# Turning an expert's rows with VectorE's 32x32 blocks and a quadrant exchange by DMA, instead of TensorE's transposes

## What is computed

```python
xn = layernorm(x)
# routing: 8 of 32 experts for each token, at most CAP = 512 slots an expert
buf = zeros(E * CAP + 1, H).at[slot].set(xn[tok])
xe = buf[:E * CAP].reshape(E, CAP, H)                  # 32 x 512 x 256
gu = einsum('ech,eoh->eco', xe, gate_up_proj)          # o = 2 * 128
g, u = minimum(gu[..., :128], 7), clip(gu[..., 128:], -7, 7)
ye = einsum('eci,ehi->ech', silu(g) * u, down_proj)
...
out = x + attention(xn) + routed(ye) + shared(xn)
```

## Time and profile before

| | us |
|---|---|
| median of three runs | 3135.45 (3132.16 to 3135.75) |
| the profiled execution | 3129.23 |
| its span from first to last instruction | 3127.6 |

### The profile page before, as it was taken

How to read it: one execution, slowest core, us unless ns; L and a number is a source line. 1 busy time by engine, 2 the same in 40 slices (tenths; PEclk the granted TensorE clock), 3 DMA queues, 4 the chain that set the end, 5 groups by cost and what they waited for, 6 DMA issues and landing times.

```text
span 3127.6 us, 54519 instructions
## 1 busy us (share of the span) xinstructions
PE 3068.8 (98%) x13443; PEld 1592.7 (51%) x13444; DVE 2624.5 (84%) x2773; ACT 1963.5 (63%) x3797; POOL 2102.4 (67%) x2156
## 2 busy tenths in 40 slices
PE   8999999999899999999999999999999999999998
PEld 3355444555455555555555555555555555555554
DVE  9622444334999999999999999999999999999995
ACT  5511420334677777777777777777777777777775
POOL 5877773011577777777777777777777777777776
PEclk9999999999999999999999999999999999999999
DMA  9821887665888888898888888988898888888887
GB/s 350 331 88 55 310 266 179 204 228 187 229 205 219 217 223 221 220 221 225 218 218 217 219 216 213 262 219 223 220 223 219 221 219 224 211 220 220 206 215 182
DMA packets 319034, 685.21 MB, mean 219 GB/s; under 512 B 120813, under 2 KB 170744, under 8 KB 318608
## 3 DMA queue, kind: packets, MB, share of 16 engines
q1 hardware_dynamic: 289808, 626.48, 76.0%
q0 software_dynamic: 29184, 58.22, 5.8%
HBM read 198.37 MB, written 159.51 MB: 114 GB/s over the span
## 4 chain that ended last, share of the span: by engine, by line
PE 69%; DMA 2%; SPq 2%; DVE 1%; issue 0%; ACT 0%; POOL 0%; DVEq 0%; ACTq 0%; POOLq 0%
PE ea_ps L1155 28%; PE ea_ps L1187 26%; PE ea_ps L1202 9%; PE ea_ps L1168 6%; DMA ea_moved<-ea_blocks 2%; SPq L976 1%; DVE ea_half_max L1282 1%; DVE ea_blocks L1299 1%; DMA out<-ahead_acc 0%; SPq L819 0%; ACT ea_scaled L1249 0%; ACT ea_prob L1237 0%; SPq L826 0%; SPq L959 0%; DVE ea_neg_max L1287 0%
## 5 line engine op out<-in xcount | busy, mean ns | idle before, releaser
L1237 ACT ACTIVATE ea_prob<-ea_ps,ea_neg_max 128x1024 f32<-128x1024 f32 x1024 | 1149.1, 1122 | 313.8 <-DVE ea_neg_max L1287 292.4
L1282 DVE TENSOR_REDUCE ea_half_max<-ea_ps 128x1 f32<-128x1024 f32 x1024 | 1201.8, 1215 | 8.5 <-PE ea_ps L1155 7.4
L1299 DVE STREAM_TRANSPOSE ea_blocks<-ea_prob 128x1792 f32<-128x1792 f32 x512 | 1043.1, 2037 | 2.9 <-DMA ea_moved<-ea_blocks 1.2
L1093 POOL COPY ea_moved<-ea_blocks 32x1792 f32<-32x1792 f32 x512 | 857.1, 1674 | 158.5 <-DVE ea_blocks L1299 49.0
L1155 PE MATMUL ea_ps<-ahead_k_hl,ahead_q_hh 128*128 128x512 f32 x2048 | 852.9, 416 | 12.7 <-ACT ea_prob L1237 12.2
L1187 PE MATMUL ea_ps<-ea_moved,ea_v 128*64 128x512 f32 x3584 | 860.0, 593 | 5.3 <-DMA ea_moved<-ea_blocks 5.2
L1155 PE MATMUL ea_ps<-ahead_k_hl,ahead_q_ll 128*128 128x512 f32 x2048 | 807.5, 394 | 0.0
L1108 POOL TENSOR_TENSOR ahead_acc<-ahead_acc,ea_scaled 128x256 f32<-128x256 f32 x512 | 375.8, 734 | 203.3 <-ACT ea_scaled L1249 67.4
L1249 ACT ACTIVATE ea_scaled<-ea_ps,ea_inv 128x256 f32<-128x256 f32 x512 | 242.2, 473 | 316.8 <-PE ea_ps L1202 312.0
L1187 PEld LDWEIGHTS ea_ps<-ea_moved,ea_v 128*64 128x64 f32 x3584 | 261.7, 137 | 351.9 <-issue 292.9
L1155 PEld LDWEIGHTS ea_ps<-ahead_k_hl,ahead_q_hh 128*128 128x128 f32 x2048 | 387.6, 189 | 85.5 <-ACT ea_prob L1237 19.5
(11 more groups left out here) (112 smaller groups left out, 2563.6 us busy)
## 6 DMA issues: line engine op xcount, KB each, us to landing
ea_moved<-ea_blocks SPq DMA_DIRECT2D x1536, 224.0 KB, 6.2
ahead_k_hl<-k_parts SPq DMA_DIRECT2D x64, 512.0 KB, 8.1
ahead_q_hh<-q_parts SPq DMA_DIRECT2D x128, 256.0 KB, 4.6
ahead_q_ll<-q_parts SPq DMA_DIRECT2D x128, 256.0 KB, 5.7
xbuf<-pr_zeros SPq DMA_DIRECT2D x32, 512.0 KB, 3.8
q_parts<-pr_part_hi SPq DMA_DIRECT2D x64, 256.0 KB, 2.4
q_parts<-pr_part_lo SPq DMA_DIRECT2D x64, 256.0 KB, 2.5
k_parts<-pr_part_hi SPq DMA_DIRECT2D x64, 256.0 KB, 2.4
```

Source lines behind the costliest of these rows:

```text
L1093: nc.gpsimd.tensor_copy(moved[r * 32:(r + 1) * 32, parity, r, :, :, :], blocks[r * 32:(r + 1) * 32, parity, r, :, :, :]).then_inc(diag_don ...
L1237: nc.scalar.activation(prob[:, i % 2, half * 1024:(half + 1) * 1024], ps[:, banks[0]:banks[1], :].rearrange("p b c -> p (b c)"), ACT.Exp, ...
L1282: nc.vector.tensor_reduce(half_max[:, i % 2, half:half + 1], ps[:, banks[0]:banks[1], :], AX.XY, ALU.max).then_inc(max_step, 1)
L1299: nc.vector.transpose(blocks[:, parity, :, j, :, :].rearrange("p c t k -> p t c k"), prob[:, (s["s"] - 1) % 2, 0:MOVED * P].rearrange("p ( ...
```

## The change

The rows of a pair are loaded by one transfer in which a partition holds four consecutive rows (`load_rows`), and the weights by `load_weights`. The first pair is still turned by TensorE. For each later pair, VectorE turns both experts' rows in 32x32 blocks into `blk` (`turn_pair`), two pairs ahead, between the pair's two `hidden` steps; SyncE sends twelve off-diagonal quadrants of `blk` to `xeT` (`exchange`), GpSimd copies the four diagonal ones (`diagonal`). `xeT` and `blk` have two places by pair. TensorE's `gate_up` waits for the weights and, in the pair's first expert, for exchange and diagonal; it reads `xeT` in runs of 32. `down` gets two banks for each place (`2 * q`), so that the attention's first scores wait for expert 30's copy. Loops run over two pairs a turn, with two pairs ahead and two behind written out.

```diff
+def load_rows(sp, scr, ahead, i):
+    sp.dma_start(ahead["xe"][:, :, :, :], scr["xbuf"][bass.ds(i * 2 * CAP, 2 * CAP), :]
+                 .rearrange("(q p t) d -> p q t d", p=P, q=2)).then_inc(ahead["xe_loaded"], 16)
...
     def sync(sp):
...
+        def exchange(i, b):
+            wait_apart(sp, blk_done, i, sp_waits)
+            wait_apart(sp, gu_ready, 2 * (i - 1), sp_waits)
+            for turn in range(1, QD):
+                for a, r in zip(ACROSS, ACROSS[turn:] + ACROSS[:turn]):
+                    sp.dma_start(xeT[r * 32:(r + 1) * 32, b, a, :, :, :, :],
+                                 blk[a * 32:(a + 1) * 32, b, r, :, :, :, :]).then_inc(exchanged[b], 16)
+
+        def body(i, b):
+            if follows(i, 2):
+                wait_apart(sp, blk_done, i + 1, sp_waits)
+                load_rows(sp, scr, ahead, i + 2)
+            if follows(i, 1):
+                exchange(i + 1, 1 - b)
+                for q in range(2):
+                    wait_apart(sp, gu_ready, 2 * i + q + 1, sp_waits)
+                    wait_apart(sp, dn_kept, 2 * i + q + 1, sp_waits)
+                    load_weights(sp, io, ahead, 2 * i + 2 + q, q)
+
+        sp.wait_ge(turned, 2)
+        load_rows(sp, scr, ahead, 1)
         for part in range(2):
             load_k(sp, scr, start, 0, 0, 0, part)
         load_q(sp, scr, start, 0, 0, 0)
-        with sp.Fori(1, E // 2) as i:
-            load(i)
+        over_pairs(sp, body)
     def gpsimd(pool):
+        def diagonal(i, b):
+            wait_apart(pool, blk_done, i, pool_waits)
+            wait_apart(pool, gu_ready, 2 * (i - 1), pool_waits)
+            for r in range(QD):
+                nc.gpsimd.tensor_copy(xeT[r * 32:(r + 1) * 32, b, r, :, :, :, :],
+                                      blk[r * 32:(r + 1) * 32, b, r, :, :, :, :]).then_inc(diag_done, 1)
...
+        def body(i, b):
+            if follows(i, 1):
+                diagonal(i + 1, 1 - b)
+            if not isinstance(i, int) or i:
+                store(i - 1)
...
+    def vector(dve):
+        def turn_pair(i, b):
+            dve.wait_ge(xe_loaded, 16 * i + 16)
+            if not isinstance(i, int) or i > 2:
+                dve.wait_ge(exchanged[b], SENT // 2 * (i - 2 + b))
+                dve.wait_ge(diag_done, QD * (i - 2))
+            for q in range(2):
+                last = nc.vector.transpose(blk[:, b, :, q, :, :, :].rearrange("p r t k j -> p (t k) r j"),
+                                           xe[:, q, :, :].rearrange("p t (k r j) -> p (t k) r j", r=QD, j=32))
+            last.then_inc(blk_done, 1)
...
+        def body(i, b):
+            hidden(i, 0)
+            if follows(i, 2):
+                turn_pair(i + 2, b)
+            hidden(i, 1)
+
+        turn_pair(1, 1)
+        over_pairs(dve, body)
     def tensor(pe):
-        def gate_up(i, q):
+        def gate_up(i, q, b):
             n = 2 * i + q
-            pe.wait_ge(xeT_done, n + 1)
+            pe.wait_ge(w_loaded[q], 32 * i + 32)
+            if isinstance(i, int) and i == 0:
+                pe.wait_ge(xeT_done, q + 1)
+            elif q == 0:
+                pe.wait_ge(exchanged[b], SENT // 2 * (i + b))
+                pe.wait_ge(diag_done, QD * i)
             wait_pos(pe, up_done, n - 1)
...
-            wait_pos(pe, ye_done, n)
+            wait_pos(pe, ye_done, n - 1)
             for t in range(CT):
-                last = nc.tensor.matmul(ps[:, 2 + t // 2, (t % 2) * D:(t % 2 + 1) * D],
+                last = nc.tensor.matmul(ps[:, 2 * q + t // 2, (t % 2) * D:(t % 2 + 1) * D],
                                         hid[:, q, t * P:(t + 1) * P], dn_old[:, q, :], start=True, stop=True)
             last.then_inc(down_ready, 1)
+        def body(i, b):
+            for q in range(2):
+                if not isinstance(i, int) or i:
+                    down(i - 1, q)
+                gate_up(i, q, b)
+
         for q in range(2):
-            turn(0, q)
-            gate_up(0, q)
...
+            turn(q)
+        over_pairs(pe, body)
...
@@ -1142,6 +1202,8 @@
+                if isinstance(tile, int) and tile == 0:
+                    pe.wait_ge(ye_done, E - 1)
```

More of the change, by code:

```diff
@@ L639, in experts_programs @@
     CT = CAP // P
-    xe, gu, dn, loaded = (ahead[name] for name in ("xe", "gu", "dn", "loaded"))
+    PAIRS = E // 2
+    SENT = QD * (QD - 1) * 16
+    xe, gu, dn, xe_loaded, w_loaded = (ahead[name] for name in ("xe", "gu", "dn", "xe_loaded", "w_loaded"))
     room = moved[:, :, :, :, :, :].rearrange("p a r j t k -> p (a r j t k)")
+    size = 2 * QD * 2 * CT * DK * 32
     def lines(n):
-        first = n * CAP
+        first = 2 * size + n * CAP
         return room[:, first:first + 2 * CAP].rearrange("p (q c) -> p q c", c=CAP)
-    xeT = room[:, 0:2 * DK * CAP].rearrange("p (q k c) -> p q k c", q=2, c=CAP)
-    gate, up, silu_g, hid = (lines(2 * DK + 2 * n) for n in range(4))
-    dn_old = lines(2 * DK + 8)[:, 0, :].rearrange("p (q d) -> p q d", d=D)
+    xeT, blk = (room[:, n * size:(n + 1) * size].rearrange("p (b a q t k j) -> p b a q t k j", b=2, a=QD, q=2, t=CT, k=DK)
+                for n in range(2))
+    gate, up, silu_g, hid = (lines(2 * n) for n in range(4))
+    dn_old = lines(8)[:, 0, :].rearrange("p (q d) -> p q d", d=D)
     ye = start["acc"][:, TILES // 2:, :].rearrange("p (q t) d -> p q t d", q=2)
@@ L662, in experts_programs, with over_pairs, follows @@
     sp_waits, pool_waits = m.sem("e_sp_waits"), m.sem("e_pool_waits")
-    def sync(sp):
[L665 to L671, removed]
+    def over_pairs(eng, body):
+        for i in (0, 1):
+            body(i, i)
+        with nc.Fori(1, PAIRS // 2 - 1, engines=[eng.engine]) as j:
+            for u in range(2):
+                body(2 * j + u, u)
+        for i in (PAIRS - 2, PAIRS - 1):
+            body(i, i % 2)
+    def follows(i, n):
+        return not isinstance(i, int) or i + n < PAIRS
+    def sync(sp):
+        def exchange(i, b):
[17 more added lines that the diff above has]
+        load_rows(sp, scr, ahead, 1)
         for part in range(2):
@@ L691, in scalar, with take @@
-    def scalar(act):
-        def turn(i, q):
-            n = 2 * i + q
-            act.wait_ge(turned, n + 1)
-            nc.scalar.copy(xeT[:, q, :, :], ps[:, 0:2, :]).then_inc(xeT_done, 1)
+        def body(i, b):
[3 more added lines that the diff above has]
+                store(i - 1)
+        over_pairs(pool, body)
+        store(PAIRS - 1)
+    def scalar(act):
+        def take(q):
+            act.wait_ge(turned, q + 1)
+            for k in range(DK):
+                last = nc.scalar.copy(xeT[:, 0, :, q, :, k, :].rearrange("p a t j -> p t a j"),
+                                      ps[:, 2 * q + k, :].rearrange("p (t a j) -> p t a j", a=QD, j=32))
+            last.then_inc(xeT_done, 1)
@@ L746, in tensor, with turn @@
     def tensor(pe):
[L747 to L749 removed]
+        def turn(q):
+            pe.wait_ge(xe_loaded, 16)
             for k in range(DK):
                 for t in range(CT):
[L752 removed]
+                    last = nc.tensor.transpose(ps[:, 2 * q + k, t * P:(t + 1) * P],
                                                xe[:, q, t, k * P:(k + 1) * P], keep["ident"][:, :])
```

103 lines of the change are left out of this document (41 added, 62 removed).

## The result

The changed kernel takes 3151.88 us (median of 5 runs, 3150.35 to 3154.41) where the kernel before takes 3135.75 (5 runs, 3132.16 to 3138.44): a ratio of 1.0062, with a 95% interval of 1.0051 to 1.0073. It is 16.1 us slower; the forecast was 3126.2, the range 3112 to 3142. The profiled execution of after took 3150.35 us (span 3148.7).

What follows compares the result with a forecast made beforehand. TensorE was taken to bound the expert stage; afterwards SyncE's queue would set 11.45 us a pair. Fourteen pairs fall from 177.2 to 159.8: 17.4 - 8.6 (start) + 0.4 (end) = 9.2 us won, giving 3126.2, range 3112 to 3142.

Steps and rivals of the forecast that it cites:

- TensorE's gain on an undisturbed expert: Experts' steady part: without transposes (0.87 us), TensorE needs 1.93 for down and 3.53 for gate and up.
- the first rival: SyncE's exchange: issues as cheap as plain loads, 0.38 us each, TensorE the bound at 10.92 a pair; 3116 us, chance 0.20.
- The end: Last experts before the attention: the last down no longer waits for its bank; 0.4 us won.
- The start: First pairs: TensorE idles 7.7 us for pair 1's exchange and weights, then a slow gate-up; loss 8.6 us.
- The forecast's own loop of two pairs: SyncE's queue: weights behind the exchange land at E + 13.9; two pairs take 22.9 us, a pair 11.45.
- I take 0.64: SyncE's exchange: 0.64 us from one quadrant issue to the next, twelve 7.7 us; bounds 0.38 and 0.69.
- two small loads take 1.12 from issue to issue: SyncE's loads around the exchange: 1.12 us for two steps, used to place weights and rows in the pair.
- It is covered, with 0.4 us to spare.: VectorE: the pair's turn, 2.4 us between the hidden halves, ends at 5.05, before the second gate-up's end at 5.46.
- Full, but under 11.45.: DMA engines: rows, weights, stores and exchange sum to 9.7 to 10.9 us a pair, within the 11.45.
- The clock: TensorE after idling at the start: low granted clock, so pair 1's first gate-up is given 7.0 us.
- The fourth: Rival: weights land late, 5.7 us, behind the exchange; a pair takes 12.75, total 3148 us; chance 0.16.
- The third: Rival: DMA engines bind, the exchange takes 4.1 us, a pair 12.0; 2.1 us won, 3133 us; chance 0.10.

Runs made afterwards that it cites:

- k3: The changed kernel with rows loaded between the two experts' weights, six of twelve transfers from ScalarE, a quarter of each result store: 3117.9 us (before 3132.4).
- e1: The changed kernel with six of a pair's twelve exchange transfers issued from ScalarE's queue instead of SyncE's: 3147.0 us (before 3127.4).
- g3: e1 with only a quarter of each store of the experts' results: 3136.8 us (before 3131.7).
- g1: The changed kernel with only a quarter of each store of the experts' results, in as many issues: 3130.0 us (before 3132.2).
- k2: The changed kernel with rows loaded between the two experts' weights and six of twelve transfers issued from ScalarE: 3129.7 us, ratio 0.9993 to before.
- f1: The changed kernel with rows loaded by GpSimd, ahead of its diagonal copies, instead of by SyncE behind the weights: 3157.0 us (before 3133.6).
- k1: The changed kernel with SyncE's next rows load moved between the first and the second expert's weights: 3139.6 us (before 3132.4).
- e4: The changed kernel with each of the twelve transfers cut in two, 24 of 32 KB, same bytes: 3257.3 us (before 3127.4).
- i1: The kernel before the change with its expert loops rewritten, two pairs in the body and four written out, same work and order: 3141.4 us, ratio 1.0028.
- m1: k2 with pairs 0 and 1 both turned by TensorE, and keys and queries loaded ahead of the rows: 3132.6 us, ratio 0.9994 to before.

## Why the prediction was wrong

**Right.** TensorE's gain on an undisturbed expert (5.16 us, 5.46 forecast; 0.2 of the rest is that gate-up no longer waits for ScalarE's copy, which ended at 667.59 where the gate-up of the earlier trace rows began at 667.65: the copy was not quite the nothing that it was costed at). The issue of a quadrant (592 ns for 598) and so the failure of the first rival. The weights' landing (3.1 us), and that TensorE waits for weights queued behind the exchange: the products at 579.84 and 606.87 start 2.5 and 3.1 us after the second of the two weight loads was issued (577.37 and 603.73); only the wait is 0.8 to 4.25 us in ten pairs and not half a microsecond in each. The turn (2.37 for 2.4). The end: from the last-but-one down to the first score 4.25 us, 4.70 before: 0.45 won for 0.4. The start: 34.4 us for 27.3, a loss of 7.1 for 8.6, with a hole of 7.22 us and a slow product behind it, as the step said. In k3, where all that the forecast took for covered is covered (with a quarter of the stores), the pair is even below its 10.92.

**Wrong: the pair, 13.33 for 11.45; 186.6 us for the 14 pairs in place of 159.8.** That is 26.8 us, more than the whole miss of 25 (9.2 won against 16.1 lost). The forecast's own loop of two pairs can be laid on the trace, with E = 590.42. Set begins at E + 2.9 (2.45 forecast); it stands 9.39 us (7.65); the second weight load is issued at E + 13.3 (10.8), lands in 3.1 (3.1), so gate-up starts at E + 16.45 (13.9); it takes 5.23 us (3.53); the end of the second pair is at E + 26.84 (22.9). Of the 3.9 us, 2.5 are SyncE's and 1.7 the clock's; the down and the second gate-up give 0.3 back. Three steps behind that failed:

- *"I take 0.64", "two small loads take 1.12 from issue to issue".* The median was right, the mean was not: with some issues held, a set takes 8.97 us, 0.75 from issue to issue, more than the attention's 0.69 that the text called a bound; and the rest takes 3.44 where the five loads of the text, at 0.56 each, give 2.8. By the text's own figures SyncE's work is 10.5 us a pair and fits in 11.45; at the measured 12.4 it does not. So this term was mis-sized: it was priced by the median issue, and the held ones make the mean.
- *"It is covered, with 0.4 us to spare."* The turn was costed by its own 2.4 us and never by what it waits for. The rows' landing stood in the start alone (5.3 us there, 5.0 measured; 8.3 in the pairs). Written out in the pair, issue to landing to turn to copy to weights to rows is 13.3 us in the stretch shown, above the forecast; with a landing of 5.3 it would have fitted, so here a wait was left out and its main term grew under load. The text even named the copy as "what would be late next", but didn't follow it to the queue behind it, where the rows themselves stand. This step alone keeps the pair above before's 12.66: e1, with SyncE relieved, took 12.93, and g3 shows the loop bare.
- *"Full, but under 11.45."* The engines' sum of 9.7 to 10.9 was close (11.2 measured), but a resource used for 0.84 of the time isn't only a bound; it lengthens each landing on the two loops beside it. g1 takes 2 us from it and gives 1.2 us a pair back, through both.

**The clock** was given to the start alone. In after's pairs the products behind the six holes of 2.4 us and more had a granted clock of 0.50 to 0.69 in their first 2.5 to 3.3 us and cost 13.2 us in all; behind the four of 1.73 and less it was 1.00. In k3, whose holes in the pairs are 1.1 us at most, it stayed at 1.00. The length of a hole alone doesn't settle it: in k2 a slow product followed one of 2.05 us, in e1 none followed one of 2.75.

**The rivals.** The fourth had the right sign and nearly the right time (3148, a pair of 12.75), by a mechanism that isn't there: weights behind the exchange landed in 3.1 us, not 5.7. It appears in f1, by another way (6.0). The third (engines bind, a pair of 12.0) is what remains in k2, at 11.76 us. The Trainium skill's rule on ports ("SBUF — State Buffer", section "Door 1: The DMA port swizzle") was weighed there; the 265 and 297 GB/s of after's and k2's windows neither bear it out nor refute it, since loads, stores and quadrants run together.

## What to carry to other kernels

When a covered engine's slack is spent, write the whole loop for each buffer that goes round (issue, landing, each engine's order, back to the issue), and compare every loop and every queue's sum with the new period, not with the old one. Size each landing for the load that the changed kernel will have. If two or three come out close together, taking one away shows little (0.4 us of a pair's 13.3 in e1, 0.6 in k1, 1.6 in k2 with both); open them together before calling any of them innocent. A transfer moved to another queue can lose the protection that its place in the first one gave its neighbours (weights in 6.0 us for 3.1 in f1).

## What the runs showed of the hardware

An issue of a 32-partition transfer between partitions of SBUF cost SyncE 0.51 us at least and 0.59 in the median whether it carried 32 or 64 KB (e4, after). With a second issuing engine (e1) a set stood 4.15 us on SyncE instead of 9.0, but the quadrants landed in 6.1 us instead of 4.1. A kernel's time moved by 9 us (i1) through the shape of loops that do the same work, over 1200 us ahead of where most of it was paid; so differences of a few us between programs of different code, k2's and m1's against before among them, say little about the work in them.
